# A two-layer transformer on one core: the middle tokens of the last attention group go first, and their feed-forward is interleaved with the outer tokens' attention

## The chip, the cores and the metric

The kernel runs on one core of one Trainium2 chip. The metric is the device time of one execution in microseconds (us). The program is written by hand for five engines that run side by side and meet at semaphores: TensorE (matrix products), VectorE (reads the accumulator memory PSUM and SBUF), ScalarE (activations, copies, and its own queue of loads), GpSimd (called POOL in the profile, SBUF only) and SyncE (here only a queue of DMAs).

## The reference, cut to what matters

The input is x, 1024 tokens of 256 channels. Two layers follow. The change touches the end of the second one:

```python
# second layer: causal attention, 32 query heads on 8 key/value heads, head size 64
x = x + _L1_attn_ref(_layernorm(x), wq, wk, wv, wo)
# its feed-forward: two "bit linear" products with ternary weights and a gelu between them
def bitlinear(x, w):
    xn = layer_norm(x)                      # (x - mean) / sqrt(var + 1e-6), token by token
    gamma = max(|xn|, axis=-1)
    x_hat = clip(xn * 128 / gamma, -128 + eps, 128 - eps) * gamma / 128
    return einsum('bsd,od->bso', x_hat, ternary(w))
h = gelu(bitlinear(layer_norm(x), w_fc))    # 256 -> 1024
x = x + bitlinear(h, w_proj)                # 1024 -> 256
```

(The source calls _layernorm ahead of the feed-forward as well.) Attention mixes tokens, and causally: a token needs only the keys up to its own. The feed-forward works token by token, so a token whose attention output is complete over all heads can go on without the others.

## The kernel before

Tokens lie in eight tiles of 128. The second layer's attention is done in eight groups (NG = 8, one key/value head and its four query heads each), and a group in eight steps, G = 0 to 63 in all (`of_step`). Before, a group takes query pair p = 0 in its first four steps and p = 1 in the last four; the step's r = 0 to 3 says which query tiles it does: tile 4 + r against its 5 + r blocks of keys (part 0) and tile 3 - r against its 4 - r blocks (part 1). So r = 0 and 1 cover the middle tiles 4, 3, 5 and 2, r = 2 and 3 the outer tiles 6, 1, 7 and 0, and each step has 9 blocks for each of two heads, 18 in all.

In a step TensorE computes the scores, VectorE their row maximum (`row_max`), ScalarE the exponentials (`exp_unit`) and their float16 high part (`p_high`), POOL the low part (`p_low`, L478), and SyncE's queue transposes both by DMA (L382, L386). Three steps later (PV_LAG = 3) TensorE multiplies the transposed probabilities with the values (`pv`, L1433 and L1437), and VectorE divides by their sum (`normalise_o`). Between these stand side jobs, given by a table (`JOBS`): projections of the next group, transposes of the attention output (`ot0` to `ot3`; 0 and 1 for p = 0, 2 and 3 for p = 1; `oT_high` on ScalarE, `oT_low` on VectorE) and the output projection of the group before (`wo0` to `wo3`, one for each pair of token tiles: 12 matmuls of 256 columns, 6 to a token tile; added to x by `add_out`). Each side job has one of two PSUM banks, in the order of the list `RING`; a job waits until VectorE has emptied the one two places ahead of it.

After step 63 the tail begins. The last three `pv` are done, `ot2` and `ot3`, and the output projection of the last group in the order 1, 2, 0, 3. Then comes the feed-forward:

- Mean and variance of each tile (`tile_moments`), in two halves of four tiles. `quantise`: subtract the mean, take the absolute maximum, its reciprocal, scale, clip: y.
- TensorE transposes y (`x_transposes(3, ...)`, L1170), ScalarE takes the high part (`x_high`), VectorE the low part (`y_low`).
- For each token tile t, in order: `fc(t)`: 8 matmuls of 512 columns. `gelu_of(t)` on ScalarE with the sum over the row. POOL turns it into a mean (`z_mean`), ScalarE subtracts it (`centre`, gives z) and adds up the squares (`squares`). VectorE takes the maximum of z and scales z by it (L1134 to L1138). `z_transposes(t)` on TensorE (L1541), `z_high` on ScalarE, `z_low` on VectorE (L1119). `pj(t)`: 16 matmuls of 256 columns. `result(t)`: scaled and added to x, and stored.

z, gelu and the PSUM banks of fc have two buffers each; the bank pair of the transposed z has one, so `z_transposes(t + 1)` waits for `z_low(t)`. Every engine runs its instructions strictly in the order in which they are written, so the order written out in each engine's block is the schedule. TensorE's, before:

```python
for t in range(NT):
    if t + 2 < NT:
        fc(t + 2)
    z_transposes(t)
    if t >= 1:
        pj(t - 1)
```

Of the kernel before, what the change touches and what calls it, by code (L numbers as in the profile page):

```python
# [31 lines left out]
def transformer_program(nc, x_in, wq_a, wk_a, wv_a, wo_a, w_gate_up, w_down,  # L32
# [97 lines left out]
    y = sb("y", 26, [NT, C], F32)  # L130
    yT_hi = sb("yT_hi", 34, [KC, T], F16)
# [33 lines left out]
    with ExitStack() as ctx:  # L165
# [21 lines left out]
        wo_landed = sem("wo_landed")  # L187
# [53 lines left out]
        y_done = sem("y_done")  # L241
# [23 lines left out]
        def of_step(G):  # L265
            g, n = G // 8, G % 8
            return g, n, n // 4, n % 4

        def blocks(G, part):
            r = G % 4  # L270
            return 4 - r if part else 5 + r
# [13 lines left out]

        def owner(G, name):
# [4 lines left out]
            return g if name[:2] in ("ot", "q1") or name[:1] == "v" else g + 1  # L291

        def job(G, slot):
# [3 lines left out]
            name = (JOBS if G >= 8 else RAMP_JOBS)[G % 8][slot]  # L297
# [7 lines left out]
        RING += [(STEPS, "pv"), (STEPS + 1, "pv"), (STEPS + 1, "ot2"), (STEPS + 2, "pv"), (STEPS + 2, "ot3")]  # L305
# [28 lines left out]
        def o_cols(oT, m):  # L334

            o = oT[:, m // 2, :]
            if m % 2:
                return o.rearrange("p (a n) -> p a n", a=4)[:, 0::3, :]
# [6 lines left out]
        def _(sp):  # L345
# [48 lines left out]
            for t in range(NT):  # L394
                sp.wait_ge(result_done, t + 1)
                sp.dma_start(out_dram[:, t, :], x[:, t, :]).then_inc(out_stored, 16)
# [4 lines left out]
        def _(pool):  # L401
# [53 lines left out]
            def split_wo_low(g):  # L455
                pool.wait_ge(wo_hi_done, g + 1)
                nc.gpsimd.tensor_tensor(wo_lo[:], wo_nat[:], wo_hi[:].bitcast(F32), ALU.subtract).then_inc(wo_split, 1)
# [32 lines left out]
            for G in range(STEPS):  # L490
# [37 lines left out]
        def _(act):  # L528
# [1070 lines left out]
```

## Time and profile before

| what | value |
|---|---|
| time, median of 3 runs | 632.26 us (629.54 to 632.45) |
| the profiled execution, its own time | 630.89 us |
| its span in the profile | 628.9 us |
| TensorE (matmul) busy | 563.0 us, 90% |
| VectorE busy | 461.7 us, 73% |
| ScalarE busy | 434.7 us, 69% |
| POOL busy | 450.0 us, 72% |
| busy from 164 to 550 us (386 us, the attention): TensorE, VectorE, ScalarE, POOL | 357, 297, 330, 356 us |
| busy from 550 to 583 us (33 us): the same | 20, 18, 4, 11 us |
| busy from 583 to 629 us (46 us): the same | 38, 35, 36, 8 us |

The profile follows one execution. Its times count from the start of the span. Busy time is that of the records of an engine. What waits for what is inferred from the semaphores. A granted clock of 1.00 is TensorE's full speed of 2.4 GHz and 0.50 is 1.2 GHz.

### The profile page before, as it was taken

What the parts mean: (1) busy time and instruction counts of PE and PEld (TensorE: products, weight loads), DVE (VectorE), ACT (ScalarE), POOL (GpSimd) and SP (SyncE); (2) the same over time, 40 slices, a digit from 0 to 9 for tenths busy, and PEclk for the clock granted to TensorE, in tenths of its full rate; (3) what the DMA queues carried; (4) which work ended last, traced back from release to release, by engine and by line L of the source; (5) the groups of instructions that cost most, each with busy time, mean ns of one, the idle gap of its engine ahead of it and who ended that gap; (6) DMA issues with size and microseconds to landing.
All of it is one profiled execution on the core that took longest, in us unless ns stands there. A gap on an engine that the chain in (4) does not pass through costs nothing.

```text
span 628.9 us, 16324 instructions
## 1 busy us (share of the span) xinstructions
PE 563.0 (90%) x6880; PEld 484.8 (77%) x6880; DVE 461.7 (73%) x764; ACT 434.7 (69%) x601; POOL 450.0 (72%) x373
## 2 busy tenths in 40 slices
PE   5999999987889999999999999999999868774896
PEld 4878888966678888888888888888889757663475
DVE  4686757767768878878877887887888756519696
ACT  0624311268788898889879889888888897701894
POOL 3033436529989998998998999999999787724121
PEclk9999999999999999999999999999999999966799
DMA  9160004009999999999999999999999999950001
GB/s 288 49 200 0 2 22 88 2 22 164 192 171 196 183 197 193 188 194 215 191 190 190 199 205 193 193 187 190 192 199 193 184 191 207 186 108 0 1 26 43
DMA packets 317192, 91.75 MB, mean 146 GB/s; under 512 B 305984, under 2 KB 316224, under 8 KB 317120
## 3 DMA queue, kind: packets, MB, share of 16 engines
q1 hardware_dynamic: 311680, 86.66, 79.3%
q10 hardware_dynamic: 5440, 4.06, 2.4%
q8 instruction: 54, 0.88, 0.5%
q14 instruction: 18, 0.15, 0.1%
HBM read 13.11 MB, written 1.05 MB: 23 GB/s over the span
## 4 chain that ended last, share of the span: by engine, by line
PE 33%; POOL 23%; DVE 13%; DMA 13%; SPq 6%; ACT 6%; issue 5%; POOLq 0%; ACTq 0%; DVEq 0%
POOL p_lo L478 17%; PE PS L1154 11%; DMA pT_lo<-p_lo 10%; DVE small L1006 4%; PE PS L1413 4%; SPq L382 4%; PE PS L1287 3%; POOL roped L467 3%; SPq L386 3%; DMA pT_hi<-p_hi 2%; PE PS L1264 2%; PE PS L1269 2%; PE PS L1265 2%; ACT probs L656 2%; PE PS L1433 2%
## 5 line engine op out<-in xcount | busy, mean ns | idle before, releaser
L478 POOL TENSOR_TENSOR p_lo<-probs,p_hi 128x1280 f16<-128x1280 f32 (+7 forms) x128 | 303.6, 2391 | 35.2 <-DMA pT_lo<-p_lo 20.5
L656 ACT ACTIVATE probs<-PS,small 128x640 f32<-128x640 f32 (+7 forms) x256 | 173.6, 743 | 43.2 <-DVE small L1006 40.1
L1006 DVE TENSOR_REDUCE small<-PS 128x2 f32<-128x1280 f32 (+7 forms) x128 | 172.8, 1351 | 22.7 <-PE PS L1413 22.1
L665 ACT CAST p_hi<-probs 128x1280 f16<-128x1280 f32 (+7 forms) x128 | 145.4, 1159 | 4.8 <-DMA pT_hi<-p_hi 4.7
L1433 PE MATMUL PS<-v_hi,pT_hi 128*128 128x65 f16 x1152 | 78.9, 195 | 1.6 <-DMA pT_hi<-p_hi 1.6
L1437 PE MATMUL PS<-v_lo,pT_hi 128*128 128x64 f16 x1152 | 78.9, 195 | 0.0
L1433 PEld LDWEIGHTS PS<-v_hi,pT_hi 128*128 128x128 f16 x1152 | 74.1, 99 | 3.3 <-issue 1.1
L1413 PE MATMUL PS<-k_hi,q_hi 64*128 64x512 f32 (+3 forms) x384 | 74.0, 381 | 1.2 <-ACT probs L656 1.2
L1437 PEld LDWEIGHTS PS<-v_lo,pT_hi 128*128 128x128 f16 x1152 | 72.6, 98 | 0.4
L1413 PE MATMUL PS<-k_hi,q_lo 64*128 64x512 f32 (+3 forms) x384 | 66.1, 339 | 0.0
L1413 PE MATMUL PS<-k_lo,q_hi 64*128 64x512 f32 (+3 forms) x384 | 66.0, 339 | 0.0
L1433 PE MATMUL PS<-v_hi,pT_lo 128*128 128x65 f16 x1152 | 46.5, 195 | 8.0 <-DMA pT_lo<-p_lo 7.9
L1154 PE MATMUL PS<-wkq_hi,xnT_hi 128*128 128x320 f32 x128 | 43.8, 342 | 8.5 <-DVE t_sin L954 3.0
L1433 PEld LDWEIGHTS PS<-v_hi,pT_lo 128*128 128x128 f16 x1152 | 40.0, 99 | 9.1 <-DMA pT_lo<-p_lo 9.1
L442 POOL TENSOR_TENSOR hT_lo<-h,hT_hi 128x512 fp32r<-128x512 f32 x16 | 23.6, 1476 | 32.7 <-DVE hT_hi L866 32.7
L467 POOL TENSOR_TENSOR roped<-t_cos,t_sin 128x256 f32<-128x256 f32 x64 | 47.0, 734 | 0.0
L1154 PE MATMUL PS<-wo_hi,oT_hi 128*128 128x256 f32 x128 | 39.8, 311 | 7.1 <-DVE oT_lo L1021 4.7
L1413 PEld LDWEIGHTS PS<-k_hi,q_hi 64*128 64x128 f32 x384 | 36.1, 184 | 12.8 <-ACT probs L656 2.0
L1399 PE MATMUL PS<-masked,picked 128*128 128x128 bf16 x256 | 36.2, 223 | 8.7 <-ACT probs L656 7.2
L1154 PE MATMUL PS<-wkq_lo,xnT_hi 128*128 128x320 f32 x128 | 39.6, 309 | 0.0
L1399 PEld LDWEIGHTS PS<-masked,picked 128*128 128x128 bf16 x256 | 16.6, 97 | 29.8 <-issue 15.7
L1154 PE MATMUL PS<-wkq_hi,xnT_lo 128*128 128x320 f32 x128 | 39.5, 308 | 0.0
(188 smaller groups left out, 1330.6 us busy)
## 6 DMA issues: line engine op xcount, KB each, us to landing
wgu_nat<-L_ffn_w_gate_up SPq DMA_DIRECT2D x2, 1024.0 KB, 9.6
wo_nat<-L_attn_wo ACTq DMA_DIRECT2D x8, 256.0 KB, 3.4
wkq_nat<-L_attn_wq ACTq DMA_DIRECT2D x6, 256.0 KB, 4.2
x<-L_attn_x SPq DMA_DIRECT2D x4, 256.0 KB, 3.8
wdn_nat<-L_ffn_w_down SPq DMA_DIRECT2D x1, 1024.0 KB, 11.3
wfc_nat<-L_ffn_w_fc SPq DMA_DIRECT2D x1, 1024.0 KB, 6.7
wpj_nat<-L_ffn_w_proj SPq DMA_DIRECT2D x1, 1024.0 KB, 9.7
pT_hi<-p_hi SPq DMA_TRANSPOSE x64, 5.6
```

The lines of the kernel that those rows point to most:

```text
L382: sp.dma_start(pT_hi[G % 3][:], p16_hi[G % 2][:], transpose=True).then_inc(pT_hi_landed[G % 3], 16)
L442: nc.gpsimd.tensor_tensor(hT_lo[:, n, :], h32[:, n % 3, :], hT_hi[:, n, :].bitcast(F32), ALU.subtract).then_inc(h_lo_done, 1)
L467: nc.gpsimd.tensor_tensor(roped[:, t, P:3 * P], t_cos[b][:, 1:5, :].rearrange("p h d -> p (h d)"), t_sin[b][:, 1:5, :].rearrange("p h d -> ...
L478: nc.gpsimd.tensor_tensor(p16_lo[G % 2][:, cols], probs[G % 2][:, cols], p16_hi[G % 2][:, cols], ALU.subtract).then_inc(p_lo_done, 1)
L656: nc.scalar.activation(probs[G % 2][:, start:start + w], PS[:, src:src + w], ACT.Exp, bias=nmax[:, 4 * (G % 2) + u:4 * (G % 2) + u + 1]).t ...
L665: nc.scalar.copy(p16_hi[G % 2][:, cols], probs[G % 2][:, cols]).then_inc(p_hi_done, 1)
L1006: nc.vector.tensor_reduce(nmax[:, first:first + 2], both_heads(G, part), AX.X, ALU.max, negate=True).then_inc(nmax_done, 1)
L1154: last = nc.tensor.matmul(dst, lhsT, rhs, start=n == 0, stop=n == len(pairs) - 1)
L1399: ended = nc.tensor.matmul(b[:, at % BANK:at % BANK + P], picked[:], masked[:], start=start, stop=stop, skip_group_check=True)
L1413: last = nc.tensor.matmul(dst[a], q[rows_of[a], q_cols], k[rows_of[a], cols], start=m == 0 and not (part == 0 and ends), stop=m == 2 and n ...
L1433: last = nc.tensor.matmul(o[:, u:u + HEAD + 1], p_block, v_hi[:, j, g, :], start=first, stop=False, skip_group_check=True)
L1437: nc.tensor.matmul(o[:, u:u + HEAD], p_block, v_lo[:, j, g * HEAD:(g + 1) * HEAD], start=False, stop=False, skip_group_check=True)
```

## The change

In the last group `of_step` gives another order: steps 56 to 59 do the middle tiles for both pairs of heads, steps 60 to 63 the outer ones. Another table of side jobs (`LAST_JOBS`) holds for this group: the projection of group 6 goes in the order 1, 2, 0, 3 in steps 59 to 62, and in step 63 stand `ot1` and then the last group's projection for the middle tokens (`po1`, `po2`). The last group's wo has its own buffers, and is loaded and split earlier: its low part on POOL in step 59 and not in step 63.

The feed-forward's tiles are numbered anew (`TAIL_TILES`): t = 0 to 3 are the middle tiles 2, 3, 4, 5, and t = 4 to 7 the outer ones 0, 1, 6, 7. After step 63 the order is written out on each engine: the first half's moments and y come right after `po2`, and the last three `pv`, `ot2`, `ot3`, `po0` and `po3` stand between fc, gelu and z work of tiles 0 to 3. Work moves from VectorE to POOL: the scaling of z (`z_quantise`), a small factor of the result (`z_factor`), and the second half's centring (`y_centre`, 4 tiles). POOL takes the reciprocal root of four variances at a time (`rstd_half`). An empty gelu call on ScalarE loads its table after the last p_high. For tiles 4 to 7, TensorE has `z_transposes(t)` ahead of `fc(t + 2)`. The split of wo on ScalarE moves with that on POOL, and load_wo of the last group to step 56. The functions `fc`, `z_transposes` and `pj` on TensorE stay as they are but for pj's bank, which is now one of `RING`, and fc's waits on PSUM.

```diff
-    wo_nat = sb("wo_nat", 69.5, [2, C], F32)
-    wo_hi = sb("wo_hi", 71.5, [2, C], F32R)
-    wo_lo = sb("wo_lo", 73.5, [2, C], F32R)
+    wo_nat = [sb("wo_nat", 69.5, [2, C], F32), sb("wo_nat_last", 75.5, [2, C], F32)]
+    wo_hi = [sb("wo_hi", 71.5, [2, C], F32R), sb("wo_hi_last", 64.5, [2, C], F32R)]
+    wo_lo = [sb("wo_lo", 73.5, [2, C], F32R), sb("wo_lo_last", 67, [2, C], F32R)]
...
+            if g == NG - 1:
+                return g, n, n // 2 % 2, 2 * (n // 4) + n % 2
...
+        LAST_JOBS = {0: ("q1t0", "q1t1", ""), 1: ("", "", "ot2"), 2: ("", "", ""), 3: ("ot3", "wo1", ""),
+                     4: ("wo2", "", ""), 5: ("ot0", "wo0", ""), 6: ("wo3", "", ""), 7: ("ot1", "po1", "po2")}
+        LAST_WO = (1, 2, 0, 3)
+        TAIL_TILES = (2, 3, 4, 5, 0, 1, 6, 7)
+
+        def wo_count(gg, j):
+
+            return 4 * gg + (LAST_WO.index(j) if gg >= NG - 2 else j) + 1
...
+            name = (RAMP_JOBS if G < 8 else LAST_JOBS if G >= STEPS - 8 else JOBS)[G % 8][slot]
...
-        RING += [(STEPS, "pv"), (STEPS + 1, "pv"), (STEPS + 1, "ot2"), (STEPS + 2, "pv"), (STEPS + 2, "ot3")]
+        RING += [(STEPS, "pv"), (STEPS, "ot2"), (STEPS + 1, "pv"), (STEPS + 2, "pv"), (STEPS + 2, "ot3"),
+                 (STEPS + 2, "po0"), (STEPS + 2, "po3")] + [(STEPS + 3, f"pj{t}") for t in range(NT)]
...
-                if n == 2 and g:
+                if n == (1 if g == NG - 1 else 2) and g:
                     split_wo_low(g - 1)
-                if G == STEPS - 1:
-                    split_wo_low(NG - 1)
+                if n == 3 and g == NG - 1:
+                    split_wo_low(g)
...
-            for i in range(NT):
-                rstd(3, i, BIT_EPS)
+            def rstd_half(hf):
+
+                v = moments[:, 3, 8 * hf + 1:8 * hf + 8:2]
+                pool.wait_ge(moments_done, 3 * NT + 4 * hf + 4)
+                nc.gpsimd.tensor_scalar(v, v, BIT_EPS, None, ALU.add).then_inc(var_eps_done, 1)
+                pool.wait_ge(var_eps_done, 2 * NT + hf + 1)
+                nc.gpsimd.tensor_tensor(v, v, neg_half.broadcast_to([P, 4]), ALU.pow).then_inc(rstd_done, 1)
...
+            def y_centre(t):
+                pool.wait_ge(moments_done, 3 * NT + t + 1)
+                nc.gpsimd.tensor_scalar(y[:, t, :], x[:, TAIL_TILES[t], :], mean_of(3, t), None,
+                                        ALU.subtract).then_inc(y_centred, 1)
...
+            def z_quantise(t):
+
+                pool.wait_ge(z_inv_done, t + 1)
+                nc.gpsimd.tensor_scalar(z[:, t % 2, :], z[:, t % 2, :], bit[:, 6, t:t + 1], Q_B, ALU.mult,
+                                        ALU.min).then_inc(z_done, 1)
+
+            def z_factor(t):
+                z_rstd(t)
+                pool.wait_ge(z_rstd_done, t + 1)
+                nc.gpsimd.tensor_scalar(bit[:, 7, t:t + 1], bit[:, 5, t:t + 1], bit[:, 10, t:t + 1],
+                                        ngam[:, 1:2], ALU.mult, ALU.mult).then_inc(z_factor_done, 1)
+
+            rstd_half(0)
+            z_mean(0)
+            z_mean(1)
+            z_quantise(0)
+            z_factor(0)
+            z_quantise(1)
+            z_mean(2)
+            z_factor(1)
+            for t in range(4, NT):
+                y_centre(t)
+            z_quantise(2)
+            z_mean(3)
+            rstd_half(1)
+            z_factor(2)
+            z_quantise(3)
+            z_factor(3)
+            for t in range(4, NT):
                 z_mean(t)
-                if t:
-                    z_rstd(t - 1)
-            z_rstd(NT - 1)
+                if t > 4:
+                    z_factor(t - 1)
+                z_quantise(t)
+            z_factor(NT - 1)
...
+            nc.scalar.activation(col(58), s_sum[:, 0:1], ACT.Gelu)
...
+            oT_high(NG - 1, 2, side_bank(STEPS, "ot2"))
             gelu_of(0)
             centre(0)
+            gelu_of(1)
+            squares(0)
+            centre(1)
+            oT_high(NG - 1, 3, side_bank(STEPS + 2, "ot3"))
+            z_high(0)
+            gelu_of(2)
+            squares(1)
+            centre(2)
+            z_high(1)
+            gelu_of(3)
+            squares(2)
+            centre(3)
+            z_high(2)
             for c in range(KC):
-                x_high(3, 1, c, 6 + c)
-            for t in range(NT):
-                if t:
-                    centre(t)
+                x_high(3, 1, c, 2 + c)
+            squares(3)
+            z_high(3)
+            gelu_of(4)
+            for t in range(4, NT):
+                centre(t)
                 if t + 1 < NT:
                     gelu_of(t + 1)
-                if t:
+                if t > 4:
                     z_high(t - 1)
                 squares(t)
             z_high(NT - 1)
...
+            def z_largest(t):
+
                 dve.wait_ge(z_centred, t + 1)
                 step(nc.vector.tensor_reduce(bit[:, 4, t:t + 1], z[:, t % 2, :], AX.X, ALU.max,
                                              apply_absolute_value=True))
                 step(nc.vector.tensor_scalar(bit[:, 5, t:t + 1], bit[:, 4, t:t + 1], 1.0 / Q_B, None, ALU.mult))
-                step(nc.vector.reciprocal(bit[:, 6, t:t + 1], bit[:, 5, t:t + 1]))
-                nc.vector.tensor_scalar(z[:, t % 2, :], z[:, t % 2, :], bit[:, 6, t:t + 1], Q_B, ALU.mult,
-                                        ALU.min).then_inc(z_done, 1)
-                if t >= 1:
-                    z_low(t - 1)
-                if t >= 2:
+                nc.vector.reciprocal(bit[:, 6, t:t + 1], bit[:, 5, t:t + 1]).then_inc(z_inv_done, 1)
+
+            for t in range(4):
+                tail_moments(t)
+            for t in range(4):
+                y_centre(t)
+            quantise(0)
+            normalise_o(STEPS - 3, side_bank(STEPS, "pv"))
+            y_low(0, 4)
+            gelu_scale(0)
+            oT_low(NG - 1, 2, side_bank(STEPS, "ot2"))
+            normalise_o(STEPS - 2, side_bank(STEPS + 1, "pv"))
+            z_largest(0)
+            normalise_o(STEPS - 1, side_bank(STEPS + 2, "pv"))
+            z_largest(1)
+            oT_low(NG - 1, 3, side_bank(STEPS + 2, "ot3"))
+            add_last(0)
+            z_low(0)
+            tail_moments(4)
+            tail_moments(5)
+            add_last(3)
+            tail_moments(6)
+            tail_moments(7)
+            z_largest(2)
+            z_low(1)
+            quantise(1)
+            result(0)
+            z_largest(3)
+            z_low(2)
+            y_low(1, 2)
+            gelu_scale(1)
+            result(1)
+            z_low(3)
+            result(2)
+            z_largest(4)
+            result(3)
+            for t in range(5, NT):
+                z_largest(t)
+                z_low(t - 1)
+                if t > 5:
                     result(t - 2)
             z_low(NT - 1)
...
             side(STEPS, "pv")
+            pe.wait_ge(exp_done, 4 * STEPS)
+            x_transposes(3, 0, 4)
+            side(STEPS, "ot2")
+            fc(0)
             side(STEPS + 1, "pv")
-            side(STEPS + 1, "ot2")
-            pe.wait_ge(exp_done, 4 * STEPS)
-            out_project(NG - 1, 1, 1)
-            out_project(NG - 1, 2, 2)
+            fc(1)
             side(STEPS + 2, "pv")
+            fc(2)
             side(STEPS + 2, "ot3")
-            out_project(NG - 1, 0, 0)
-            out_project(NG - 1, 3, 3)
-
-
-            x_transposes(3, 0, 4)
-
...
-            fc(0)
-            fc(1)
-            x_transposes(3, 1, 4)
-            for t in range(NT):
+            z_transposes(0)
+            side(STEPS + 2, "po0")
+            side(STEPS + 2, "po3")
+            z_transposes(1)
+            fc(3)
+            side(STEPS + 3, "pj0")
+            z_transposes(2)
+            side(STEPS + 3, "pj1")
+            pe.wait_ge(gelu_done, 4)
+            x_transposes(3, 1, 0)
+            z_transposes(3)
+            side(STEPS + 3, "pj2")
+            fc(4)
+            fc(5)
+            side(STEPS + 3, "pj3")
+            for t in range(4, NT):
+                z_transposes(t)
                 if t + 2 < NT:
                     fc(t + 2)
-                z_transposes(t)
-                if t >= 1:
-                    pj(t - 1)
-            pj(NT - 1)
+                if t > 4:
+                    side(STEPS + 3, f"pj{t - 1}")
+            side(STEPS + 3, f"pj{NT - 1}")
```

## Rows read from the trace of the kernel before

**Rows 1.** Timeline, SyncE's queue at its end (start us, us):
```profile
551.54 2.71 SPq L382 DMA_TRANSPOSE pT_hi<-p_hi  x1
554.48 2.66 SPq L386 DMA_TRANSPOSE pT_lo<-p_lo  x1
```
**Rows 2.** Chain that ended last, in order of time (start us, us):
```profile
557.03 5.08 PE PS L1154 x24
566.72 1.69 PE PS L1154 x12
579.84 6.33 PE PS L1154 x16
...
596.28 3.47 PE PS L1154 x24
600.63 3.47 PE PS L1154 x24
```
**Rows 3.** Groups of VectorE from 566 us on (count | busy us, mean ns | idle before):
```profile
L1119 DVE SCALAR_TENSOR_TENSOR zT_lo<-PS,zT_hi 128x1024 f16<-128x1024 f32 x8 | 9.8, 1220 | 1.6 <-ACT zT_hi L713 1.6
L1134 DVE TENSOR_REDUCE bit<-z 128x1 f32<-128x1024 f32 x8 | 9.8, 1219 | 1.5 <-ACT z L728 1.1
L1138 DVE TENSOR_SCALAR z<-z,bit 128x1024 f32<-128x1024 f32 x8 | 6.0, 753 | 0.3
L1129 DVE SCALAR_TENSOR_TENSOR x<-PS,bit,x 128x256 f32<-128x256 f32 x8 | 3.9, 484 | 1.5 <-PE PS L1154 1.2
```
**Rows 4.** Groups of ScalarE from 566 us on:
```profile
L735 ACT ACTIVATE square<-gelu,bit 128x1024 bf16<-128x1024 f32 x8 | 9.2, 1155 | 0.0
L728 ACT ACTIVATE z<-gelu,bit 128x1024 f32<-128x1024 f32 x8 | 9.1, 1142 | 0.4 <-POOL bit L510 0.4
L720 ACT ACTIVATE gelu<-PS,bit 128x1024 f32<-128x1024 f32 x8 | 8.9, 1116 | 5.2 <-PE PS L1154 5.0
L713 ACT CAST zT_hi<-PS 128x1024 f16<-128x1024 f32 x8 | 8.1, 1007 | 2.7 <-PE PS L1541 2.7
```
**Rows 5.** Timeline of TensorE (in brackets the idle time before, and its releaser):
```profile
541.60 0.39 PE L1154 MATMUL PS<-wo_hi,oT_hi 128*128 128x256 f32 x1 [0.32 <-DVE oT_lo L1021]
...
548.45 1.17 PE L1433 MATMUL PS<-v_hi,pT_lo 128*128 128x65 f16 x18 [2.81 <-DMA pT_lo<-p_lo]
...
590.91 0.77 PE L1541 MATMUL PS<-identf,z 128*128 128x128 f32 x5 [2.13 <-DVE z L1138]
```
**Rows 6.** Windows (us, busy PE PEld DVE ACT POOL, granted clock, DMA, GB/s):
```profile
548.00:557.00 9.00, 5.38 (x76) 4.69 (x77) 1.91 (x5) 0.59 (x1) 5.92 (x3) 0.50 1.08 212
557.00:560.00 3.00, 2.97 (x14) 3.00 (x15) 0.00 (x0) 0.00 (x0) 0.00 (x0) 0.50 0.58 111
560.00:563.00 3.00, 3.00 (x47) 2.94 (x47) 0.00 (x0) 0.00 (x0) 0.00 (x0) 0.75 0.00 0
...
590.00:593.00 3.00, 2.09 (x12) 1.42 (x13) 2.69 (x6) 3.00 (x5) 1.39 (x3) 0.87 0.00 0
593.00:596.00 3.00, 3.00 (x12) 1.75 (x11) 2.29 (x3) 3.00 (x5) 0.75 (x2) 0.56 0.00 0
596.00:629.00 33.00, 26.96 (x211) 20.85 (x209) 26.44 (x47) 23.80 (x34) 5.61 (x17) 1.00 0.10 33
```
**Rows 7.** Timeline of ScalarE, POOL and VectorE, three places:
```profile
544.33 2.21 ACT L665 CAST p_hi<-probs 128x2048 f16<-128x2048 f32 x2
552.57 1.26 POOL L457 TENSOR_TENSOR wo_lo<-wo_nat,wo_hi 128x512 fp32r<-128x512 f32 x1
626.29 0.48 DVE L1129 SCALAR_TENSOR_TENSOR x<-PS,bit,x 128x256 f32<-128x256 f32 x1 [1.21 <-PE PS L1154]
```
**Rows 8.** Groups of POOL, whole span:
```profile
L478 POOL TENSOR_TENSOR p_lo<-probs,p_hi 128x1024 f16<-128x1024 f32 x16 | 34.3, 2146 | 0.0
L516 POOL TENSOR_SCALAR bit<-bit 128x1 f32<-128x1 f32 x8 | 1.5, 192 | 14.8 <-ACT square L735 14.8
L425 POOL CAST picked<-identf 128x128 bf16<-128x128 f32 x1 | 0.3, 291 | 0.1
```

More of the change, by code:

```diff
@@ L717, in gelu_of @@
                 act.wait_ge(fc_done, t + 1)
+                act.wait_ge(gelu_scale_done, t // 4 + 1)
                 if t >= 2:
@@ L1056, in _ @@
             side(STEPS - 1, 2)
-            for G in range(STEPS, STEPS + PV_LAG):
-                normalise_o(G - PV_LAG, side_bank(G, "pv"))
-                if G == STEPS + 1:
-                    oT_low(NG - 1, 2, side_bank(G, "ot2"))
-                if G == STEPS + 2:
-                    oT_low(NG - 1, 3, side_bank(G, "ot3"))
             ADDS = 8 + 4 * (NG - 1)
@@ L1072, in _, with add_last, tail_moments, y_centre @@
             rstds = moments[:, 3, :].rearrange("p (i two) -> p i two", two=2)
+            def add_last(j):
+                add_out(wo_count(NG - 1, j), j, side_bank(STEPS + 2, f"po{j}"))
+            def tail_moments(t):
+                if t % 2 == 0:
+                    dve.wait_ge(x_added, ADDS + t // 2 + 1)
+                nc.vector.bn_stats(stats[:, 6 * t:6 * t + 6], x[:, TAIL_TILES[t], :]).then_inc(stats_done, 1)
+                dve.wait_ge(stats_done, 3 * NT + t + 1)
+                nc.vector.bn_aggr(moments[:, 3, 2 * t:2 * t + 2], stats[:, 6 * t:6 * t + 6]).then_inc(moments_done, 1)
+            def y_centre(t):
+                dve.wait_ge(moments_done, 3 * NT + t + 1)
+                nc.vector.tensor_scalar(y[:, t, :], x[:, TAIL_TILES[t], :], mean_of(3, t), None,
+                                        ALU.subtract).then_inc(y_centred, 1)
             def quantise(hf):
                 tiles = slice(4 * hf, 4 * hf + 4)
-                dve.wait_ge(moments_done, 3 * NT + 4 * hf + 4)
-                for i in range(4 * hf, 4 * hf + 4):
-                    last = nc.vector.tensor_scalar(y[:, i, :], x[:, i, :], mean_of(3, i), None, ALU.subtract)
-                    if i < 4 * hf + 3:
-                        steps[0] += 1
-                        last.then_inc(bit_step, 1)
-                step(last)
+                dve.wait_ge(y_centred, 4 * hf + 4)
                 step(nc.vector.tensor_reduce(bit[:, 0, tiles], y[:, tiles, :], AX.X, ALU.max,
@@ L1088, in quantise, with gelu_scale, y_low @@
                 step(nc.vector.reciprocal(bit[:, 2, tiles], bit[:, 1, tiles]))
-                for i in range(4 * hf, 4 * hf + 4):
-                    nc.vector.tensor_scalar(y[:, i, :], y[:, i, :], bit[:, 2, i:i + 1], Q_B, ALU.mult,
+                for t in range(4 * hf, 4 * hf + 4):
+                    nc.vector.tensor_scalar(y[:, t, :], y[:, t, :], bit[:, 2, t:t + 1], Q_B, ALU.mult,
                                             ALU.min).then_inc(y_done, 1)
-                dve.wait_ge(rstd_done, 2 * NT + 4 * hf + 4)
+            def gelu_scale(hf):
+                tiles = slice(4 * hf, 4 * hf + 4)
+                dve.wait_ge(rstd_done, 2 * NT + hf + 1)
                 nc.vector.scalar_tensor_tensor(out=bit[:, 3, tiles], in0=bit[:, 1, tiles], scalar=ngam[:, 0:1],
-                                               in1=rstds[:, tiles, 1], op0=ALU.mult, op1=ALU.mult)
-            def y_low(hf):
+                                               in1=rstds[:, tiles, 1], op0=ALU.mult,
+                                               op1=ALU.mult).then_inc(gelu_scale_done, 1)
+            def y_low(hf, b):
                 for c in range(KC):
@@ L1384, in scores @@
                     pe.wait_ge(qk_lo_done, 6 * g + 4)
-                if n == 4 and part == 0:
+                if n == (2 if g == NG - 1 else 4) and part == 0:
                     pe.wait_ge(qk_lo_done, 6 * g + 6)
```

140 lines of the change are left out of this document (69 added, 71 removed).

## Prediction

> **What bounds the kernel now.** I read the queue of the transposing DMAs first. Through the last attention group SyncE's queue issues back to back: the reader is to see that each issue starts where the one before ended, 551.54 + 2.71, then 554.48 [rows 1]. A step of attention therefore costs what two such transposes cost, some 6.2 us, whichever q tiles it holds (18 blocks of 128 keys in every step). The softmax engines run ahead of it, and at the end it drains: the last matrix product over the probabilities is ready only about 559.5, 5 us after the last issue (the DMA engines are still busy in 557 to 560 and not after, [rows 6]).
>
> Then I read the chain that ended last. From 596.28 it repeats every 4.35 us, once for each of the eight feed-forward tiles: 3.47 us of fc and pj products and 0.88 us of transposes on TensorE [rows 2]. VectorE spends 1.22, two small steps and 0.75 on a tile's scaling, 1.22 on z_low and 0.48 on its result, with a small factor before it [rows 3], ScalarE 1.12 + 1.14 + 1.16 + 1.01 (each overlaps the next by about 0.1) and two short accumulator reads [rows 4]: all three engines are nearly full, so all of them bound this stage. But between 545 and 596 nothing is: TensorE waits 2.81 us for a landing [rows 5], and in the windows its granted clock is 0.50 from 548 to about 561 and again later [rows 6]. fc(0) starts at 579.84, 25 us after the last transpose was issued. The change reaches into this hole.
>
> **Part by part, to the first fc.** Steps of the last group: the same 18 blocks, the same matmuls. wo2 and wo3 now come ahead of pv and hold it up by 1.55 us in steps 60 and 62 (12 matmuls took 1.69 with their tail, [rows 2]). Hidden: the probabilities of the last step were cast by 546.5 [rows 7] and their transpose was issued at 551.54, 5 us later. Without that cover it would cost 3 us. Splitting wo's last rows (POOL, 1.26 us between the two parts of step 63, [rows 7]) moves to step 59, where POOL idles for a landing. POOL ends its last p_lo 1.26 us earlier; the last issue can move by only 0.23 us, the gap in SyncE's queue [rows 1]. I count the group at 0, with 0 to +3 as bounds.
>
> The two middle out-projections, po1 and po2, stand where wo3 and ot1 stood: from 541.60 [rows 5], 2 x 1.55, and the second add ends at 545.7. Before, the out-projection ended at 568.4 and fc(0) began 11.4 us later [rows 2]; 2.9 of these were the other half's add and moments on VectorE, which now come later. In their place are one normalise_o (0.6) and one more add to wait for. Step by step, with what these stages took between 569.2 and 575.5 before (2.1, 1.2, 1.7 and 1.2 us): moments 547.8, centring 549.0, absolute maximum and reciprocal 550.7, y 551.9, normalise 552.4, transposes and casts at half clock 553.9, y_low 554.6. So fc(0) starts at 554.7, not 579.84: 25 us earlier. Only a part of this can be kept, since 554.7 lies ahead of the landing of the last probabilities.
>
> **From there to the end,** each time the later of what the instruction waits for and its place in its engine's order, with the durations of [rows 2 to 4]. I take the clock as 1.00 from 558.5.
> TensorE: fc(0) ends 558.3 (3.6 at half clock), pv(62) 560.0, fc(1) 561.7, pv(63) 563.5, fc(2) 565.2, ot3 565.6, z transposes of tile 0 566.5. po0 needs oT_low, which VectorE reaches at 567.6 behind tile 1's maximum: 567.7, po3 ends 570.8. VectorE's z_low(0) is queued behind po0's add and ends 571.2, so z(1) 571.2 to 572.1, fc(3) 573.9, pj0 575.6. ScalarE: gelu(2) 567.6, centre(2) 569.9, gelu(3) 574.0.
> VectorE then has z_largest(2) behind po3's add and moments 6 and 7 (574.1 to 575.7), z_low(1) 576.8, the second half's quantise 579.6, result(0), z_largest(3) 581.7, z_low(2) 582.9, y_low(1) 584.1. TensorE meanwhile: z(2) 576.9, pj1 579.5, second y transposes 580.4, an idle 2.5 us until z(3) at 582.9, pj2 585.5, fc(4) 587.2, fc(5) 589.0, pj3 590.7.
> fc(4) thus starts at 585.5. Before it stood in the 3.47 us that begin at 596.28, behind the 16 matmuls of pj0 [rows 2], so at about 597.9: 12.4 us are won here, and half of the 25 is given back to queueing in the mixed stretch.
> The last four tiles: gelu(4) 587.4, centre(4) 588.9 to 590.0, maximum 591.7, quantise on POOL 592.8, z(4) 592.8. Here the new order costs. It puts z_transposes(t) ahead of fc(t+2), while ScalarE keeps gelu(t+2) ahead of z_high(t): z (0.9) then fc (1.75) then gelu (1.2) then z_high (1.0) then z_low (1.2) are in one circle of 6.1 us, against 4.35 before. It runs twice: z(5) 599.0, z(6) 605.1. With no fc left z(7) follows at 608.8, z_high 611.0, z_low 612.2, pj7 614.2, result 614.7. Before, the last result ended at 626.77 [rows 7]: 12.0 us earlier.
>
> **POOL's new work.** Its z_quantise (one input, 1024 columns) has no row. Nearest below: its one-input CAST of 128 columns, 291 ns, against 192 ns for one column, so about 0.8 ns a column and 1.05 us; nearest above: the two-input p_lo of 1024 columns, 2.15 us [rows 8]. The sums above take 1.05, by the row that has one input too. With 2.15 the waits on it at tiles 2 and 3 add 2.0 (z_mean(3) is queued behind z_quantise(2)), at z(4) 1.1 and at z(7) 1.1: 4.2 us. POOL's overlap with VectorE's y work before 552 may hold up its last p_lo; the cover is 558.4 - 554.9 for gelu_scale.
> The Trainium skill (GPSIMD Engine Reference, Engine selection) holds one-input work on GpSimd to be roughly line-rate and two-input work about 2x slower than VectorE, but names VectorE for elementwise work all the same. The two rows agree with the first half; 4.2 us is what this case would lose if z_quantise ran at the second.
>
> **The clock.** In the rows it fell to 0.50, the lower of its two levels (1.2 of 2.4 GHz), after TensorE had idled 2.81 us before 548.45, and around 592 to 595.6 (0.87, then 0.56) after an idle of 2.13 us before 590.91 [rows 5, 6]; it came back only in dense work (0.75 in 560 to 563, behind the 5.08 us of out-projections that began at 557.03). The new order has idle stretches of 2.5 (580), 2.1 (591) and 3.5 us (595.5), and several of 1 to 2. fc costs 3.4 instead of 1.75 at half clock, z 0.9 more. A low stretch of 3 us thus costs about 1.6, and I charge two of them: 3.2. Bounds: 0 (low only beside waits) and 22 (all chained TensorE work after 565 low).
> The Trainium skill (TensorE: Matmul & The Clock Gate, HAM oscillation) says of such bursts separated by waits that they bring the clock down again and again. By that rule this change could eat its gain; its outcome is the slower rival below, and the trace bears the fall out after each of the two gaps.
>
> **Sum.** -12.0 + 3.2 + 0 = -8.8 against the profiled execution of 630.89 (span 628.9, 2.0 around it): 622.1. The three runs' median is 632.26, lowest 629.54; I say 622.
>
> **Rivals.** (a) *POOL is slow*: z_quantise at 2.15; for it only the two-input row, against it CAST. 622 + 4.2 = 626. (b) *The clock holds*: z and fc are dense enough, 596 to 629 at 1.00 with gaps of 1 to 1.5 us speaks for it, the 3.5 us gap against: 619. (c) *The group stretches*: wo2 and wo3 in front of pv delay row_max by 1.55 twice: 625. Against it: 5 us of cover. (d) *Slower*: the clock stays at 0.50 through the mixed stretch and the last tiles. It costs up to 22 us; over 12 of these, so low for more than half of TensorE's chained work after 565, the change loses. At all 22: 641. Against it: at half clock the same work fills TensorE, and dense work brought the clock back. (e) *It does nothing*: the middle tokens wait for something bound to the last step after all and fc(0) starts near 570 with the work as dense as before: 630. Against it: every wait ahead of fc(0) that I followed ends by 554.6.
>
> **Chances.** Forecast 622 (620 to 624): 0.46. (a) 0.20. (b) 0.16. (c) 0.08. (d) 0.05. (e) 0.05. The range reaches from (b) less 2 to (a) plus 2: 617 to 628. This measurement can't tell less than about 0.5%, 3.2 us, from nothing; faster 0.90, within 0.05, slower 0.05.
>
> **What would show it.** fc(0) starting at 554 to 556; SyncE's last issue still near 554.3; fc(4) at 585 to 588; z transposes of tiles 4, 5, 6 spaced by about 6.1 us and the last two by under 4.5; z_quantise at 1.05 us; a granted clock of 0.50 in one or two stretches after 575. The prediction is wrong if SyncE's last issue comes after 556, if z_quantise is near 2 us, or if the clock is low for 10 us in the last 50.

## The result, and the profile after

The changed kernel is slower: 638.89 us (637.35 to 640.01, 4 runs) against 631.6 us (629.54 to 632.45, 4 runs), a ratio of 1.0122 with a 95% interval of 1.0098 to 1.0147. Forecast were 622 us and a range of 617 to 628. The profiled execution took 638.03 us, its span is 636.2.

SyncE's queue ends where it did, as the timeline of the kernel after shows (before: [rows 1]); attention is not longer.

```profile
552.02 2.70 SPq L396 DMA_TRANSPOSE pT_hi<-p_hi  x1
554.76 2.78 SPq L400 DMA_TRANSPOSE pT_lo<-p_lo  x1
```

The chain that ended last looks different from [rows 2]. Pieces of it, kernel after, in order of time (start us, us; those between are left out):

```profile
548.51 5.26 DVE y L1163 x4
559.48 1.89 PE PS L1267 x8
566.28 3.71 POOL z L550
571.37 3.69 POOL z L550
576.66 3.62 POOL y L532 x4
580.27 3.74 POOL z L550
587.13 3.73 POOL z L550
592.00 3.49 PE PS L1267 x24
599.95 3.73 POOL z L550
603.73 1.97 PE PS L1635 x8
605.69 2.54 PE PS L1267 x8
611.77 1.94 PE PS L1635 x8
613.71 3.43 PE PS L1267 x8
623.18 3.72 POOL z L550
```

POOL was nowhere in the tail of the chain before. Now z_quantise (L550) stands in it six times at 3.7 us (tiles 0 to 4 and 7), and the second half's centring (L532) once. Where VectorE needed 0.75 us for the same scaling (L1138 in [rows 3]), the groups of POOL after show five times that:

```profile
L550 POOL TENSOR_SCALAR z<-z,bit 128x1024 f32<-128x1024 f32 x8 | 29.8, 3722 | 7.4 <-DVE bit L1216 7.3
L532 POOL TENSOR_SCALAR y<-x,moments 128x256 f32<-128x256 f32 x4 | 3.6, 928 | 0.0
```

The chain's first row is the other surprise. Four centrings of 256 columns (L1163), which took 1.1 us together before, take 5.3. The view of that line (min/median/max in ns) shows that one of them does it, and the timeline of POOL what ran beside it (two instructions, of 2048 and 256 columns):

```profile
L1163 DVE TENSOR_SCALAR y<-x,moments x4: 323/550/4150, 548.4 to 553.4; 128x256 f32<-128x256 f32 x4
```
```profile
548.45 4.89 POOL L495 TENSOR_TENSOR p_lo<-probs,p_hi 128x2048 f16<-128x2048 f32 x2 [2.74 <-ACT p_hi L730]
```

The transposes of z come far apart. TensorE after, tile 2 and then tiles 4 to 6 (idle time before in brackets):

```profile
584.07 1.97 PE L1635 MATMUL PS<-identf,z 128*128 128x128 f32 x8 [4.39 <-POOL z L550]
...
603.73 0.69 PE L1635 MATMUL PS<-identf,z 128*128 128x128 f32 x2 [4.78 <-POOL z L550]
...
611.77 1.94 PE L1635 MATMUL PS<-identf,z 128*128 128x128 f32 x8 [3.55 <-DVE zT_lo L1197]
...
620.67 1.07 PE L1635 MATMUL PS<-identf,z 128*128 128x128 f32 x8 [1.59 <-DVE zT_lo L1197]
```

From tile 4 on the spacings are 8.0 and 8.9 us where 4.35 was the rule before and 6.1 was forecast. Windows show how busy each engine is meanwhile (us, busy PE PEld DVE ACT POOL, granted clock, DMA share, GB/s). In 576 to 590 POOL is the full engine, 13.31 of 14 us, TensorE waits 4.39 us for it, and the mean granted clock is 0.76:

```profile
559.00:576.00 17.00, 13.91 (x176) 10.71 (x177) 9.36 (x21) 10.73 (x16) 9.74 (x10) 0.99 0.00 1
576.00:590.00 14.00, 9.61 (x54) 7.16 (x53) 9.71 (x21) 5.84 (x8) 13.31 (x14) 0.76 0.03 11
590.00:606.00 16.00, 11.02 (x72) 7.94 (x71) 6.28 (x11) 8.84 (x13) 7.18 (x10) 0.93 0.07 25
606.00:622.00 16.00, 10.86 (x52) 6.51 (x51) 5.53 (x10) 8.80 (x13) 10.05 (x10) 0.75 0.02 6
```

### The profile page after: what moved, and what is told of

It is laid out like the page before. It is cut to its first block, busy times and chain, and to the rows that moved or that the text cites. A ratio compares the mean times of both kernels' runs of the same rounds, so it can differ in the third digit from the quotient of the medians.

```text
span 636.2 us, 16317 instructions
## 1 busy us (share of the span) xinstructions
PE 566.9 (89%) x6880; PEld 487.3 (77%) x6880; DVE 457.3 (72%) x744; ACT 435.4 (68%) x602; POOL 481.8 (76%) x381
## 3 DMA queue, kind: packets, MB, share of 16 engines
HBM read 13.11 MB, written 1.05 MB: 22 GB/s over the span
## 4 chain that ended last, share of the span: by engine, by line
PE 41%; POOL 20%; DVE 17%; DMA 7%; ACT 7%; SPq 4%; issue 4%; ACTq 0%; POOLq 0%; DVEq 0%
PE PS L1267 12%; POOL p_lo L495 11%; PE PS L1526 7%; DVE small L1088 7%; DMA pT_lo<-p_lo 6%; POOL z L550 4%; PE PS L1546 3%; PE PS L1400 3%; ACT probs L721 3%; SPq L396 2%; PE PS L1377 2%; PE PS L1382 2%; PE PS L1378 2%; POOL roped L484 2%; SPq L400 2%
## 5 line engine op out<-in xcount | busy, mean ns | idle before, releaser
L495 POOL TENSOR_TENSOR p_lo<-probs,p_hi 128x2048 f16<-128x2048 f32 (+7 forms) x128 | 303.8, 2392 | 35.3 <-ACT p_hi L730 18.8
L721 ACT ACTIVATE probs<-PS,small 128x128 f32<-128x128 f32 (+7 forms) x256 | 173.8, 744 | 44.4 <-DVE small L1088 42.1
L1088 DVE TENSOR_REDUCE small<-PS 128x2 f32<-128x2048 f32 (+7 forms) x128 | 172.9, 1351 | 21.8 <-PE PS L1526 21.2
L730 ACT CAST p_hi<-probs 128x2048 f16<-128x2048 f32 (+7 forms) x128 | 145.8, 1160 | 6.1 <-DMA pT_hi<-p_hi 6.0
L1526 PEld LDWEIGHTS PS<-k_lo,q_hi 64*128 64x128 f32 x384 | 36.8, 187 | 3.5
L1526 PEld LDWEIGHTS PS<-k_hi,q_lo 64*128 64x128 f32 x384 | 36.8, 187 | 2.7
```

What stands on the lines that cost most here:

```text
L495: nc.gpsimd.tensor_tensor(p16_lo[G % 2][:, cols], probs[G % 2][:, cols], p16_hi[G % 2][:, cols], ALU.subtract).then_inc(p_lo_done, 1)
L721: nc.scalar.activation(probs[G % 2][:, start:start + w], PS[:, src:src + w], ACT.Exp, bias=nmax[:, 4 * (G % 2) + u:4 * (G % 2) + u + 1]).t ...
L730: nc.scalar.copy(p16_hi[G % 2][:, cols], probs[G % 2][:, cols]).then_inc(p_hi_done, 1)
L1088: nc.vector.tensor_reduce(nmax[:, first:first + 2], both_heads(G, part), AX.X, ALU.max, negate=True).then_inc(nmax_done, 1)
L1526: last = nc.tensor.matmul(dst[a], q[rows_of[a], q_cols], k[rows_of[a], cols], start=m == 0 and not (part == 0 and ends), stop=m == 2 and n ...
```

## Experiments

Theory A: the cost is what POOL takes for the scaling. Theory B: the written-out interleaving itself costs, by queueing. Each run was measured beside the kernel before, on the same chip: experiments 1 to 6, 8 and 9 on one chip (kernel before 631.35 for 1 to 4, 631.15 for the others), 7 and 10 to 12 on another (631.74). Ratios are to the kernel before, with a 95% interval. Microseconds between two versions of different groups lean on these three medians being within 0.1% of each other.

### 1. The kernel before, with z scaled on POOL

```diff
-                step(nc.vector.reciprocal(bit[:, 6, t:t + 1], bit[:, 5, t:t + 1]))
-                nc.vector.tensor_scalar(z[:, t % 2, :], z[:, t % 2, :], bit[:, 6, t:t + 1], Q_B, ALU.mult,
-                                        ALU.min).then_inc(z_done, 1)
+                nc.vector.reciprocal(bit[:, 6, t:t + 1], bit[:, 5, t:t + 1]).then_inc(z_inv_done, 1)
...
                 if t:
                     z_rstd(t - 1)
+                pool.wait_ge(z_inv_done, t + 1)
+                nc.gpsimd.tensor_scalar(z[:, t % 2, :], z[:, t % 2, :], bit[:, 6, t:t + 1], Q_B, ALU.mult,
+                                        ALU.min).then_inc(z_done, 1)
```

> The kernel before, with one part of the change alone: z is scaled on POOL and not on VectorE. Theory A (POOL's price is the cause; 3.72 us for an instruction where VectorE took 0.75): a tile's circle becomes centre 1.15, maximum and two small steps 1.6, scaling 3.7, z_mean of the next tile 0.2, so about 6.8 us against 4.35, and seven such periods add 17 us: 645 to 650. Theory B (the written-out interleaving of attention and feed-forward costs, POOL's price is hidden beside it): the old order has slack for it, under 635.

Measured: 652.16 us against 631.35, ratio 1.032 (1.0288 to 1.0351): 21 us slower, from this one part. Its chain repeats every 6.83 us, as worked out (6.8):

```profile
611.17 1.23 DVE bit L1137
612.89 3.71 POOL z L525
618.01 1.23 DVE bit L1137
619.72 3.71 POOL z L525
```

The traces of both tell the 4 us over the expected 17. From the first scaling to the last it is 47.8 us against 28.7 before, so 19.1 more (before, the first two scalings follow each other in 2.6 us and not in 4.35), and from the start of the last scaling to the last result 9.75 against 7.98, 1.8 more. Theory A holds for the old order.

### 2. The changed kernel, with z scaled on VectorE

POOL's calls of `z_quantise` go, and its `z_factor` waits for the scaling; on VectorE:

```diff
-                nc.vector.reciprocal(bit[:, 6, t:t + 1], bit[:, 5, t:t + 1]).then_inc(z_inv_done, 1)
+                step(nc.vector.reciprocal(bit[:, 6, t:t + 1], bit[:, 5, t:t + 1]))
+                nc.vector.tensor_scalar(z[:, t % 2, :], z[:, t % 2, :], bit[:, 6, t:t + 1], Q_B, ALU.mult,
+                                        ALU.min).then_inc(z_done, 1)
```

> The changed kernel with one part taken back: z is scaled on VectorE again, right after its maximum; all else as changed. Theory A: six scalings stand on the chain that ended last, each 3.0 us shorter, so 636 - 17 + 2 = 619 to 625, faster than before. Theory B: 633 or more.

Measured: 629.82 us, ratio 0.9979 (0.9958 to 1.0). That lies between what the two theories gave. It takes 9.1 us off the changed kernel, not the 17 of "six times 3.0": with POOL out of the chain, other waits end last. So A is right in kind and too large in size, and something besides is missing, since 622 was forecast for a scaling of 1.05 us. The chain shows two more things, the same slow centring, and z(5) to z(6) still 7.7 us apart:

```profile
548.75 4.64 DVE y L1159 x4
```
```profile
606.56 1.94 PE L1633 MATMUL PS<-identf,z 128*128 128x128 f32 x8 [3.55 <-DVE zT_lo L1193]
...
614.26 0.41 PE L1633 MATMUL PS<-identf,z 128*128 128x128 f32 x2 [1.80 <-DVE zT_lo L1193]
```

### 3. The changed kernel, first half centred on ScalarE

VectorE only negates the four means (4 columns), and ScalarE subtracts:

```diff
-            for t in range(4):
-                y_centre(t)
+            dve.wait_ge(moments_done, 3 * NT + 4)
+            nc.vector.tensor_scalar(small[:, 36:40], moments[:, 3, 0:8:2], -1.0, None, ALU.mult).then_inc(ymean_done, 1)
             quantise(0)
...
             nc.scalar.activation(col(58), s_sum[:, 0:1], ACT.Gelu)
+            act.wait_ge(ymean_done, 1)
+            for t in range(4):
+                nc.scalar.activation(y[:, t, :], x[:, TAIL_TILES[t], :], ACT.Identity,
+                                     bias=small[:, 36 + t:37 + t]).then_inc(y_centred, 1)
```

> The changed kernel, but the first half's centring (4 instructions on VectorE, one of which took 4.15 us beside POOL's p_low) is done on ScalarE. Theory A as extended: the two engines keep each other from SBUF, so fc(0) starts about 4 us earlier (555 to 556, before 559.5), and the end moves by 2 to 4 us: 635 to 637 in time. A rival, that VectorE waited for something else there: fc(0) still after 558 and the time stays at 638 to 639. Since POOL's scaling of z is still there, neither makes it as fast as before.

Measured: 641.02 us, ratio 1.0133 (1.0102 to 1.0164). fc(0) began at 561.77, 8.1 us after the last p_hi transpose was issued, against 7.5 in the changed kernel, so the numbers of my theory failed. The trace shows why: the instruction of 4 columns on VectorE took 3.73 us, from 550.59 to 554.31, and POOL's p_low of 2048 columns ended at 554.29 (timelines of VectorE and of POOL; POOL's row holds 2048 and 256 columns).

```profile
550.37 0.18 DVE L1163 BATCH_NORM_AGGREGATE moments<-stats 128x2 f32<-128x6 f32 x1
550.59 3.73 DVE L1225 TENSOR_SCALAR small<-moments 128x4 f32<-128x4 f32 x1
```
```profile
550.23 4.68 POOL L495 TENSOR_TENSOR p_lo<-probs,p_hi 128x2048 f16<-128x2048 f32 x2 [2.46 <-DMA pT_lo<-p_lo]
```

Shared bandwidth would not do this to 4 columns: the VectorE instruction waits until the running instruction of POOL is over. ScalarE's 1.7 us then came behind the wait instead of beside it.

Two other places bound this. In the kernel before, beside POOL's two-input instruction of 68.64 to 69.92, a VectorE scaling of one column is not held and one of two columns is:

```profile
68.98 0.15 DVE L902 TENSOR_SCALAR small<-small 128x1 f32<-128x1 f32 x1
69.43 0.52 DVE L908 TENSOR_SCALAR small<-small 128x2 f32<-128x2 f32 x1
```
```profile
68.64 1.28 POOL L442 TENSOR_TENSOR hT_lo<-h,hT_hi 128x512 fp32r<-128x512 f32 x1 [1.43 <-DVE hT_hi L866]
```

And in the changed kernel four VectorE scalings of 256 columns take their usual time (0.35 us each, 1.14 together) while POOL's scaling of z runs (timelines of VectorE and of POOL):

```profile
581.98 1.14 DVE L1175 TENSOR_SCALAR y<-y,bit 128x256 f32<-128x256 f32 x4
```
```profile
580.25 3.76 POOL L550 TENSOR_SCALAR z<-z,bit 128x1024 f32<-128x1024 f32 x1
```

So it was POOL's two-input instructions that held VectorE, and not its one-input scaling. Those seen to hold it have 256 columns or more; the reciprocal root of four variances (two inputs, 4 columns, 1.04 us) does not: in experiment 10 VectorE's scalings of 256 columns beside it take 0.35 us each.

### 4. Experiments 2 and 3 together, second half centred on VectorE

> Both of these together, and the second half's centring on VectorE too, so that POOL does only its small columns after p_low. Theory A: the hand-worked schedule of the prediction with its first fc at 555, so 617 to 621. Theory B: 630 or more.

Measured: 633.5 us, ratio 1.0032 (1.0005 to 1.0058). Missed by 12 us, and 3.7 above experiment 2, with the same wait of 3.70 us on the 4-column instruction. How much of the 3.7 is the second half's centring was not measured alone.

### 5. z on POOL, in another form of instruction

```diff
-                nc.gpsimd.tensor_scalar(z[:, t % 2, :], z[:, t % 2, :], bit[:, 6, t:t + 1], Q_B, ALU.mult,
-                                        ALU.min).then_inc(z_done, 1)
+                nc.gpsimd.tensor_tensor(z[:, t % 2, :], z[:, t % 2, :], bit[:, 6, t:t + 1].broadcast_to([P, F]),
+                                        ALU.mult).then_inc(z_done, 1)
```

> The changed kernel, z still scaled on POOL but by another form of instruction: a two-input product of z with the reciprocal broadcast along the row, without the clip at +128 (only a rounding above 128 is left unclipped). If the cost is POOL's duration, time follows it: by the row of p_lo an instruction of 1024 columns takes about 2.15 us, 1.57 less than 3.72, and the six on the chain give 9 us back if each is worth what was seen when they went to VectorE (9.1 us for 2.97 each, so about 3 us for each us): 638.9 - 4.8 = 634. A rival, that it is the two handovers and POOL's queue that cost, not the duration: it stays at 637 or more.

This form leaves out the upper clip (`min` with Q_B). Measured: 629.73 us, ratio 0.9972 (0.9951 to 0.9993): 4 us under the 634 expected, and the same as with VectorE. Its group of POOL:

```profile
L550 POOL TENSOR_TENSOR z<-z,bit 128x1024 f32<-128x1024 f32 x8 | 15.2, 1894 | 8.6 <-DVE bit L1216 8.6
```

The same 1024 columns in half the time, by the form that reads two inputs. The missing `min` is not what made it short: the second half's centring (L532 above) has one operation only and still takes 0.93 us for 256 columns, 3.6 ns a column like the scaling of z. The handovers between the engines are all still there, so it was the duration that cost. Scaling in 0.75 us on VectorE, without the handovers, bought nothing more in this order; but there VectorE is full in the mixed stretch (13.52 of 14 us in 576 to 590 in experiment 2, 12.26 here).

### 6. TensorE's order for tiles 4 to 7 taken back, z on VectorE

```diff
             for t in range(4, NT):
-                z_transposes(t)
                 if t + 2 < NT:
                     fc(t + 2)
+                z_transposes(t)
```

> z on VectorE, and for tiles 4 to 7 fc(t + 2) ahead of z_transposes(t) on TensorE, as in the kernel before. If the circle z, fc, gelu, z_high, z_low is what spaces z(4), z(5), z(6) (6.4 and 7.7 us with z on VectorE), they come at 4.4 to 5 us and the time falls by 3 to 4 us, to 626. If something else spaces them (clock, VectorE's order), the spacing stays and the time is 629 to 630.

Measured: 624.23 us, ratio 0.9888 (0.9865 to 0.9911): 5.6 us less than experiment 2, more than the 3 to 4 expected, and faster than the kernel before. The transposes of tiles 5 to 7 now come every 4.2 us, and the clock is 1.00 behind 606:

```profile
605.59 1.06 PE L1633 MATMUL PS<-identf,z 128*128 128x128 f32 x8 [1.67 <-DVE zT_lo L1193]
...
609.76 1.06 PE L1633 MATMUL PS<-identf,z 128*128 128x128 f32 x8 [1.36 <-DVE zT_lo L1193]
...
613.94 1.07 PE L1633 MATMUL PS<-identf,z 128*128 128x128 f32 x8 [1.36 <-DVE zT_lo L1193]
```

### 7. The same order with z in POOL's slow form

> The changed kernel with only TensorE's order for tiles 4 to 7 taken back (fc(t + 2) ahead of z_transposes(t)); z stays on POOL in its 3.72 us form. With z on VectorE this order gave 5.6 us. Theory: the gain needs a short scaling; with 3.72 us the circle centre, maximum, scaling, z_mean of the next tile (6.8 us) takes over, so z(4) to z(7) come at 6.8 to 7.5 us and the time falls by only 0 to 3 us, 636 to 639. Rival: the two costs simply add, 633.

Measured: 636.19 us, ratio 1.0076 (1.005 to 1.0101), 2.7 us less than the changed kernel, as expected. The gains do not add: the circle over POOL stands in the way, at 6.83 us.

```profile
598.38 3.72 POOL z L550
605.22 3.71 POOL z L550
612.05 3.72 POOL z L550
```

### 8. No such VectorE instruction beside p_low, z on VectorE

As experiment 3, but ScalarE makes the negated means too (`nc.scalar.mul(small[:, 36:40], moments[:, 3, 0:8:2], -1.0)`), and z is scaled on VectorE.

> z on VectorE, and the first half centred on ScalarE with the negated mean also made there, so that VectorE issues no SBUF-to-SBUF scaling until POOL's long p_low is over. Theory (such an instruction on VectorE, however small, waits for POOL's running instruction): no VectorE instruction over 1.5 us in 548 to 556, fc(0) 5 to 5.5 us after the issue of the last p_hi transpose instead of 7.5, time 627.5. Rival (any work on y there is slow): fc(0) still 7 us after it, 629 to 630.

Measured: 627.5 us, ratio 0.9945 (0.9925 to 0.9964), the time expected. fc(0) began 5.9 us after the issue of the last p_hi transpose, not 7.5 (5 to 5.5 expected). In the timelines of VectorE and POOL of this kernel, statistics and a reduction run at their usual duration while p_low runs:

```profile
552.75 0.39 DVE L1159 BATCH_NORM_STATS2 stats<-x 128x6 f32<-128x256 f32 x1
...
555.37 1.22 DVE L1172 TENSOR_REDUCE bit<-y 128x4 f32<-128x1024 f32 x1 [2.01 <-ACT y L775]
```
```profile
552.39 4.70 POOL L495 TENSOR_TENSOR p_lo<-probs,p_hi 128x2048 f16<-128x2048 f32 x2 [1.82 <-DMA pT_lo<-p_lo]
```

### 9. to 12. Combinations

> All of these: z on VectorE, first half centred on ScalarE with its negated mean, second half centred on VectorE, fc(t + 2) ahead of z_transposes(t). If the parts add up, 624; if the second half's gain is eaten by queueing on VectorE, 626 to 627.

Experiment 9 measured: 625.44 us, ratio 0.9901 (0.988 to 0.9921): no better than experiment 6. Its fc(0) came earlier against SyncE's last p_hi issue (5.2 us behind it and not 7.7), but VectorE was full in the mixed stretch, 13.52 of 14 us:

```profile
576.00:590.00 14.00, 8.75 (x65) 6.46 (x64) 13.52 (x31) 7.61 (x11) 4.25 (x9) 0.94 0.03 11
```

> z on POOL as the two-input product (1.89 us, no upper clip) and fc(t + 2) ahead of z_transposes(t). If the two-input form is as good as VectorE and frees VectorE in the mixed stretch, 622 to 624; if POOL's queue (z_mean behind the scaling, circle 5.0 us) takes over for tiles 4 to 7, 625 to 627.

Experiment 10 measured: 625.75 us, ratio 0.9907 (0.9872 to 0.9942), the second branch. VectorE has room again (12.42 of 14 us), but the scalings of tiles 4 to 6 come every 4.98 us, the circle of 5.0 over POOL:

```profile
598.72 1.89 POOL z L550
603.70 1.89 POOL z L550
608.68 1.89 POOL z L550
```

> The same with the first half centred on ScalarE, negated mean made there, so that no VectorE scaling waits for POOL's last p_low. It took 1.6 us off fc(0) and about 2 us off the time with z on VectorE: 2 us under the run with the two-input product and the order alone. If the mixed stretch eats it again, the same as that run.

Experiment 11 measured: 623.87 us, ratio 0.9885 (0.985 to 0.9919). 1.9 us under the run before it, which is about what was expected, though the intervals overlap. With experiment 6 it is the fastest version; between these two no difference can be told.

> The same, and the second half's centring on VectorE, so that POOL (11 of 14 us busy in 576 to 590 with the two-input product) gives its 3.7 us back there: 619 to 621 if POOL's queue was the bound of that stretch, otherwise as the run before it.

Experiment 12 measured: 627.41 us, ratio 0.9941 (0.9919 to 0.9963). This expectation fell: the second half's centring on VectorE made it slower by 3.5 us, though POOL had been given room. In its trace the stretch from 576 to 590 has a clock of 0.89 where the version without it has 1.00; cause and effect were not separated there. The loss is complete at fc(4), which begins 38.7 us after the last p_hi issue and not 35.4. A part of it is again a held VectorE instruction: one of the four centrings takes 1.09 us and ends 0.15 behind POOL's two-input product of 578.00 to 579.89.

```profile
L1167 DVE TENSOR_SCALAR y<-x,moments x4: 343/344/1086, 579.0 to 580.5; 128x256 f32<-128x256 f32 x4
```

## Why the prediction was wrong, by its own steps

- **Attention at 0: right.** Steps 56 to 63 took 44.3 us from one p_hi issue to the other, against 44.5 before; SyncE's last issue came at 554.76 (forecast 554.3).
- **The first fc at 554.7: the step failed, it was 559.5.** po1 began at 542.48, 0.9 later than taken. The rest is the y work. I priced four centrings at 1.2 us by their rows from a stretch in which POOL was nearly idle, and moved them beside POOL's longest instruction. I saw the overlap and asked only whether it would delay POOL; it was VectorE that waited, 4.15 us in one instruction. Experiments 3 and 8 show that the wait ends with p_low and that statistics and reductions are not held. The trace of the kernel before had it already: the same kind of instruction in an earlier phase, mostly 0.4 us, took 1.36 us once and 1.75 us once, both times until 0.15 us after a two-input instruction of POOL.

```profile
L765 DVE TENSOR_SCALAR xn<-x,moments x24: 381/407/1745, 6.0 to 115.6; 128x256 f32<-128x256 f32 x24
```

  The Trainium skill (SBUF — State Buffer, SBUF: two separate sides) says that VectorE's two-port modes and GpSimd share one pair of ports under an exclusive lock, and that the loser waits for the whole instruction. Beside p_low the trace agrees, 3.73 us for 4 columns; beside POOL's one-input scaling of z it does not, four VectorE scalings of 256 columns ran at 0.35 us each, and there the measurement decides. Which mode VectorE was in no run shows. It would have been a rival against this change, and I had not weighed it.
- **POOL's new work at 1.05 us, 2.15 at most: the step that decided, and mis-sized.** It measured 3.72, where the prediction called near 2 us a sign that it is wrong. My lower row was a copy and my upper row another operation with two inputs; neither was a bound for a scaling with a per-row factor. The mechanism of rival (a) was right (the waits at its tiles 2, 3, 4 and 7 are in the chain, and those at tiles 0 and 1 besides), and its 4.2 us became 9.1 (experiment 2). The Trainium skill (GPSIMD Engine Reference, Engine selection) calls one-input work about line-rate and two-input work slower; here the one-input form took twice as long as the two-input one (3.72 against 1.89), and the measurement decides.
- **The circle of z, fc, gelu, z_high and z_low at 6.1 us: right in mechanism, under-sized.** With z on VectorE the spacings were 6.4 and 7.7 us, and its undoing was worth 5.6 us, not twice 1.75 (experiment 6). At half clock, z transposes take 1.94 instead of 1.06 and fc more, and both stand in the circle, so a low clock lengthens it. The best version wins 7 to 8 us in all.
- **The clock at 3.2 us: too small, and not settled alone.** After 565 the clock was at 0.50 for 20 us in four stretches (583.3 to 590.1, 603.8 to 607.2, 610.6 to 617.4, 627.7 to 631.1), 17 of them in the last 50, where the prediction took 10 as a sign that it is wrong; the kernel before has 10 in its last 50. The first of the windows with a low mean (0.76) lies where TensorE waits 4.39 us for POOL, the second (0.75) where it waits 3.55 us for VectorE in the circle; in experiment 2 these windows had 0.96 and 0.90. Against the same work at full clock, TensorE's pieces on the chain from 603.73 on are longer by about 0.9, 0.8, 0.9 and 1.7 us, and those of tile 7 by 0.3 and 0.6: some 5 us, an estimate. They are a part of the 9.1 and 5.6 us and not a term beside them. No run changes the clock alone.
- **The sum.** Attention did not end at the same time in every profiled execution: the last p_hi issue lies between 550.3 and 555.5 in the versions of the new order, though what they do up to there is the same. The tail alone, from that issue to the end of the last result, is read from one execution each (us):

| version | last p_hi issue | fc(0) | last result ends | tail |
|---|---|---|---|---|
| before | 551.54 | 579.84 | 626.77 | 75.2 |
| forecast, with 3.2 for the clock | 551.54, as before | 554.7 | 617.9 | 66.4 |
| after | 552.02 | 559.48 | 633.80 | 81.8 |
| experiment 2 (z on VectorE) | 551.60 | 559.10 | 624.76 | 73.2 |
| experiment 8 (z on VectorE, no centring held) | 555.50 | 561.37 | 624.23 | 68.7 |
| experiment 6 (z on VectorE, old order) | 552.55 | 560.20 | 619.96 | 67.4 |
| experiment 11 (two-input z, old order, no centring held) | 553.49 | 558.43 | 618.21 | 64.7 |

  The tail was 15.4 us longer than forecast, the time 16.9 (638.89 against 622). Three terms were taken away one after the other. Taking z off POOL gave 8.6 us of tail and 9.1 of time. Taking away the held centring gave another 4.5 of tail and 2.3 of time (experiments 2 and 8). The circle costs 2.3 of tail and 2.1 of time above its forecast of 3.5 (5.8 and 5.6, experiments 2 and 6). By the tails that is the whole, by the times 3.4 us stay open. The second term is the least certain: its tail is 1.6 us ahead at fc(0) and 4.4 at fc(4), and in between TensorE ran at half clock in two places in experiment 2 (until 561.6, and 588.9 to 592.3) where it did not in experiment 8, which had one such place of its own (574.6 to 578.1), while attention ended 3.9 us later in that one execution. Nor do the terms simply add: with z in POOL's slow form the old order gives 2.7 us and not 5.6 (experiment 7).
- **What is left of the change.** With z scaled in a short form and TensorE's old order, the same interleaving is 1.1% faster than before (experiments 6 and 11), at 624 us. Theory B was right in this much, that one written-out order, z_transposes ahead of fc, cost 5.6 us. Rivals (b), (c), (d) and (e) did not happen: the clock did not hold, the group kept its pace, the clock was low for 20 of the last 71 us and not throughout, and fc(0) did start 20 us earlier.

## What to carry to other kernels

A price for an operation that the trace does not show must be bounded by rows of the same engine and the same kind (number of inputs, factor per row), or the range has to stay open above; here it was 1.7 times my upper bound, and it cost 9.1 us where 8.8 were to be gained. Where an instruction moves, ask for each engine what runs beside it at its new place, and which of the two is held; the longest instances of its kind in the trace (min/median/max of its line) may already show it. And when work is interleaved to fill a hole, write down each circle of engines that one tile passes through before the next can start: it, and not the busy share, sets the pace.

## What the runs showed of the hardware that I had not expected

- GpSimd's scaling by a per-row factor with a minimum behind it: 3.72 us for 1024 float32 columns; a subtraction of a per-row mean: 0.93 us for 256; a two-input product with the factor broadcast: 1.89 us for 1024. VectorE: 0.75 us for the first.
- A VectorE scaling from SBUF to SBUF, of 256, 4 or 2 columns, that starts beside a two-input instruction of GpSimd of 256 columns or more ends just after it (0.15 us after for 256 columns, 0.03 for 4 and 2: durations of 4.15, 3.73, 3.70, 0.52 us). One column is not held (0.15), nor are VectorE's statistics (0.39) and reductions (1.22). Beside GpSimd's one-input scaling of 3.76 us, VectorE's scalings are not held either (0.35 for 256 columns). GpSimd's p_low was hardly longer than before (the 2048 and 256 columns together 4.7 to 4.9 us in all these runs).
